# GPS layer: row numbers of every chunk kept, sum buffers given back pair by pair

## The chip, the cores and the metric

The kernel runs on one core of one Trainium2 chip. The metric is the device time of one execution in microseconds (us), as a median over several runs.

## The reference, cut to what matters

A graph of 6250 nodes (256 channels) and 100000 edges, sorted by `dst`. A message network, a linear attention and a slice attention are added to the nodes. The change lies in the message network:

```
xn   = layernorm(x)
row, col = src, dst
filt = silu(edge_attr_20 @ Wf1 + bf1) @ Wf2 + bf2      # 100000 x 256
msg  = xn[col] * filt                                  # 100000 x 256
agg  = segment_sum(msg, row, num_segments=6250)        # a scatter with addition
h    = silu(agg @ Wu1 + bu1) @ Wu2 + bu2
```

## The kernel before, in words

After a first layer norm comes the long stage `messages_and_attention`. It cuts the edges into 98 chunks (`NCH`) of 1024 edges; a chunk is 8 tiles (`ET`) of 128 edges, handled as 4 pairs (`PAIRS`, index `j`). Each engine has its own program, written out by hand, and engines meet only at semaphores. For each pair:

- PE spreads rows of a loaded window of `xn` to the edges (`gather`, L654), makes the filter (`filt`, L664 and L666) and a hidden half of a later pair (`hidden`, L644).
- ACT copies the gathered rows (`copy_rows`, L874), applies silu (L848) and rounds the message to its high half (`high_half`, L867).
- DVE multiplies to the message (`message`, L1018), makes the low half (`low_half`, L981), and compares edge numbers (`indicate` L975, `equal` L993 and L994), which gives a 128x128 mask of edges of the same `src` (`same`) and each edge's rank among its equals (`rank`).
- PE multiplies message halves by the mask (`merge`, L678), so that each edge of a tile has the sum of all edges of that tile with its `src`. ACT copies this to `summed` (`copy_sums`, L855). There are two buffers `summed`, for even and odd chunks, of 8 tiles each.
- POOL adds each tile of 128 rows of 1 KB to a table in HBM with an indirect DMA (`scatter`, L610). Tile `t` goes to table `t % 2` (`TABLES`), and a scatter waits until the one before it on the same table has landed (semaphore `added[k]`, which goes up by 16 for each; `PER` = 4 scatters for each chunk and table). So one scatter per table is under way, two in all.
- The rows that a scatter adds to are in `out_idx`, one column for each tile. DVE makes them once for each chunk, at the end of the chunk before (`out_rows`, L1003 and L1009): the edge's `src`, or a row past the nodes where the edge is not the first of its equals. `src_f` holds `src` as a float, `to_trash` the distance from `src` to that spare row.
- SP loads for later pairs and chunks (`chunk` in the sync program, L503 to L526): `src_row` 512 KB and two `dst_row` of 256 KB for each chunk, a `window` of 128 KB for each pair, `attr` 120 KB for each half chunk. Each load waits until its buffer has been used, mostly by DVE or PE.

Between the pairs stand shares of the linear attention (`work(j)`): scores, gram and output passes of 7 groups. After the stage all engines meet at the block's end, and `update_nodes` begins by loading the tables.

Two places hold the messages' side back when it runs ahead of the scatters. In `out_rows` DVE waits before it writes the row numbers of chunk c until all scatters up to chunk c-2 are down, since `out_idx` has two buffers:

```
dve.wait_ge(added[k], 16 * PER * (c - 1))
```

In `copy_sums` ACT has the same wait, for the same count, before each of the four copies of chunk c, since `summed` has two buffers.

Of the kernel before, what the change touches and what calls it, by code (L numbers as in the profile page):

```python
# [16 lines left out]
I32 = mybir.dt.int32  # L17
ACT = mybir.ActivationFunctionType
X = mybir.AxisListType.X
ds = bass.ds  # L20

P = 128
# [10 lines left out]
ET = 8  # L33
# [8 lines left out]
TABLES = 2  # L42
# [280 lines left out]
def is_first(v):  # L323
    return isinstance(v, int) and v == 0
# [11 lines left out]
def messages_and_attention(nc, sem, sb, g):  # L336
# [16 lines left out]
    PER = ET // TABLES  # L353
# [6 lines left out]
    src_f = sb("src_f", [P, NCH * ET], F32)  # L360
    to_trash = sb("to_trash", [P, NCH * ET], F32)
# [6 lines left out]
    half_f = sb("half_f", [P, 1], F32)  # L368
    base_i = sb("base_i", [1, NW], I32)
    wide_i = sb("wide_i", [1, 1], I32)  # L370
    out_idx = [sb(f"out_idx{p}", [P, ET], I32) for p in range(2)]
    hidT = sb("hidT", [P, 2, CB, HE], F32)
    gathered = sb("gathered", [P, PAIRS, 2, C], F32)
    msg = sb("msg", [P, 2, 2, C], F32)
# [5 lines left out]
    redirect = sb("redirect", [P, ET], F32)  # L380
# [39 lines left out]
    out_ready = sem("e_out_ready")  # L420
    sum_made = sem("e_sum_made")
    sum_ready = sem("e_sum_ready")
    added = [sem(f"e_added{k}") for k in range(TABLES)]
# [57 lines left out]
    with nc.Block() as block:  # L481
# [108 lines left out]
        @block.gpsimd  # L590
        def _(pool):
            def gather(c, j):
                pool.wait_ge(gath_copied, PAIRS * c + j + 1)
                for t in range(2):
                    n = ET * c + 2 * j + t
                    nc.gpsimd.indirect_dma_start(
                        gathered[:, j, t, :], None, g.xn_dram,
                        bass.IndirectOffsetOnAxis(ap=dst_all[:, n:n + 1], axis=0)).then_inc(late_in[j], 16)

            def scatter(c, j):  # L600
                if j == 0:
                    pool.wait_ge(out_ready, c + 1)
                pool.wait_ge(sum_ready, PAIRS * c + j + 1)
                for t in range(2 * j, 2 * j + 2):
                    k = t % TABLES
                    if c == 0 and t < TABLES:
                        pool.wait_ge(g.table_clear[k], 16 * CLEARS)
                    else:
                        pool.wait_ge(added[k], 16 * (PER * c + t // TABLES))
                    nc.gpsimd.indirect_dma_start(  # L610
                        g.sums_dram[k], bass.IndirectOffsetOnAxis(ap=out_idx[c % 2][:, t:t + 1], axis=0),
                        summed[c % 2][:, t, :], None, compute_op=ALU.add).then_inc(added[k], 16)

            nc.gpsimd.memset(attr[:], 0.0).then_inc(cleared, 1)
            pool.wait_ge(win_step, WIN_DONE)
            is_wide = pool.value_load(wide_i[0:1, 0:1], min_val=0, max_val=1)
            with pool.If(is_wide > 0):
                gather(0, 0)
                gather(0, 1)
                for c in range(NCH):  # L620
                    for j in range(PAIRS):
                        n = PAIRS * c + j + 2
                        if n < NW:
                            gather(n // PAIRS, n % PAIRS)
                        scatter(c, j)
            with pool.Else():
                for j in range(PAIRS):
                    pool.sem_inc(late_in[j], 32 * NCH)
                for c in range(NCH):
                    for j in range(PAIRS):  # L630
                        scatter(c, j)
            for k in range(TABLES):
                pool.wait_ge(added[k], 16 * PER * NCH)
# [207 lines left out]
        def _(act):  # L841
# [8 lines left out]
            def copy_sums(c, p, j):  # L850
                act.wait_ge(sum_made, PAIRS * c + j + 1)
                if not (isinstance(c, int) and c < 2):
                    for k in range(TABLES):
                        act.wait_ge(added[k], 16 * PER * (c - 1))
                A.activation(summed[p][:, ds(2 * j, 2), :], sps[:].rearrange("p (t c) -> p t c", c=C),  # L855
                             ACT.Copy).then_inc(sum_ready, 1)

# [19 lines left out]
            def chunk(i, p, last, work):  # L877
                c = 2 * i + p
                for j in range(PAIRS):
                    if j < PAIRS - 1:  # L880
                        copy_rows(c, j + 1)
                    elif not last:
                        copy_rows(c + 1, 0)
                    if j % 2 == 0 and not last:
                        high_attr(c + 1, j // 2)
                    if j == 0:
                        silu(c, 1, 1)
                    elif not last:
                        silu(c + 1, (j - 1) // 2, (j - 1) % 2)
                    high_half(c, j)  # L890
                    if j:
                        copy_sums(c, p, j - 1)
                    elif not is_first(c):
                        copy_sums(c - 1, 1 - p, PAIRS - 1)
                    work(j)
# [59 lines left out]
            copy_rows(0, 0)  # L955
            along(act, chunk, scores, gram, output)
            copy_sums(NCH - 1, 1, PAIRS - 1)

        @block.vector
        def _(dve):  # L960
            V = nc.vector
# [37 lines left out]
            def out_rows(i, p):  # L999

                c = 2 * i + p
                dve.wait_ge(same_ready, PAIRS * c + PAIRS)
                V.scalar_tensor_tensor(out=redirect[:], in0=rank[:], scalar=0.0, in1=to_trash[:, ds(c * ET, ET)],  # L1003
                                       op0=ALU.is_gt, op1=ALU.mult).then_inc(redirected, 1)
                dve.wait_ge(redirected, c + 1)
                if not is_first(i):
                    for k in range(TABLES):
                        dve.wait_ge(added[k], 16 * PER * (c - 1))
                V.tensor_tensor(out_idx[p][:], redirect[:], src_f[:, ds(c * ET, ET)], ALU.add).then_inc(out_ready, 1)  # L1009

            def message(i, p, j):
                c = 2 * i + p
# [8 lines left out]
            def chunk(i, p, last, work):  # L1021
                c = 2 * i + p
                for j in range(PAIRS):
                    message(i, p, j)
                    if j < 2:
                        indicate(c, j + 2)
                    elif not last:
                        indicate(c + 1, j - 2)
                    if not last:
                        equal(i + p, 1 - p, 2 * j)  # L1030
                    low_half(i, p, j)
                    if not last:
                        if j % 2 == 0:
                            low_attr(c + 1, j // 2)
                        equal(i + p, 1 - p, 2 * j + 1)
                    work(j)
                if not last:
                    out_rows(i + p, 1 - p)
# [156 lines left out]
            for t in range(ET):  # L1195
                equal(0, 0, t)
            out_rows(0, 0)
            along(dve, chunk, scores, gram, output)

# [756 lines left out]
def gps_layer(nc, w, x, attr_T, src_rows, src_cols, dst_cols, dst_rows, out):  # L1956
    with ExitStack() as ctx:
# [27 lines left out]
        with ExitStack() as mixing:  # L1985
            sb_mix = lambda *a: mixing.enter_context(nc.sbuf_tensor(*a))
            g.weights = mixing_weights(sb_mix, g)
            g.gate = sb_mix("gate", [P, CB, GC], F32)
            g.zeros = g.gate[:].rearrange("p f n -> p (f n)")[:, 0:ROWS // P * C // CLEARS]
            g.table_clear = [sem(f"table_clear{k}") for k in range(TABLES)]  # L1990
            scoped(first_layernorm, g)
            g.xT = sb_mix("xT", [P, CB, NPAD], F32)
            g.k_max = sb_mix("k_max", [P, CB, 2 * NG], F32)
            g.neg_k_max = sb_mix("neg_k_max", [P, CB], F32)
            g.k_sum = sb_mix("k_sum", [P, CB, 2 * NG], F32)
            g.k_tot = sb_mix("k_tot", [P, CB], F32)
            g.k_inv = sb_mix("k_inv", [P, CB], F32)
            g.bg1f = sb_mix("bg1f", [GH, 1], F32)
            g.wg1f = sb_mix("wg1f", [P, CB, GH], F32)
            g.head_mask = sb_mix("head_mask", [P, P], F32)  # L2000
            g.wqm = sb_mix("wqm", [P, CB, C], F32)
            scoped(messages_and_attention, g)
# [46 lines left out]
```

## Time and profile before

| | us |
|---|---|
| median of 3 runs | 2826.51 |
| lowest, highest | 2817.86, 2831.32 |
| the profiled execution, its own time | 2839.35 |
| its span | 2837.6 |

| engine | busy us | share | instructions |
|---|---|---|---|
| PE | 2088.7 | 74% | 10455 |
| DVE | 1735.1 | 61% | 5026 |
| ACT | 1477.9 | 52% | 2519 |
| POOL | 1423.7 | 50% | 975 |

The shares are averages over the whole span, of which the stage with the messages is about three quarters. A POOL instruction of L610 is the issue of a DMA: its length is the time to issue it, not to land.

### The profile page before, as it was taken

Reading aid. Unit: us, or ns where it says so; the run is one execution under the profiler, and the core shown is the slowest. Engines: PE = TensorE matmul, PEld = TensorE weight load, DVE = VectorE, ACT = ScalarE, POOL = GpSimd, SP = SyncE. Lnnn points to the kernel's source line nnn. Section 1 sums busy time; section 2 is a strip of 40 time slices with the busy share of each in tenths; the row PEclk is TensorE's granted clock in tenths of the full one; section 3 lists DMA queues with packets and bytes.
Section 4 is the critical chain, followed back from the end, with each engine's and each line's share of the span. In section 5 each row is a group of like instructions: output and inputs, shape, how many; then the busy total and the mean of one; then the engine's idle time right before and its main releaser. Section 6 shows DMA issues by size and latency. Waiting matters only on the chain. (4 is left out here: it accounts for less than half of the span.)

```text
span 2837.6 us, 43386 instructions
## 1 busy us (share of the span) xinstructions
PE 2088.7 (74%) x10455; PEld 1704.5 (60%) x10455; DVE 1735.1 (61%) x5026; ACT 1477.9 (52%) x2519; POOL 1423.7 (50%) x975
## 2 busy tenths in 40 slices
PE   0187776677786877787786787878777838789979
PEld 0165665565565755666565666665656537568859
DVE  8266666565565655565665565655656625789945
ACT  1154554454654756566565575746564714346613
POOL 3155665555555565555555555555555543135510
PEclk9998898899898988899998898989898969789979
DMA  8887777777676777777777777777777763300002
GB/s 292 333 178 148 135 154 143 140 147 139 131 155 131 140 135 140 148 149 128 159 143 143 143 159 139 156 133 156 142 150 140 145 116 107 117 1 0 0 16 91
DMA packets 315000, 384.73 MB, mean 136 GB/s; under 512 B 34759, under 2 KB 256135, under 8 KB 314744
## 3 DMA queue, kind: packets, MB, share of 16 engines
q1 hardware_dynamic: 194168, 263.69, 31.8%
q0 software_dynamic: 112896, 102.81, 30.2%
q10 hardware_dynamic: 7744, 16.30, 1.5%
q14 instruction: 149, 1.22, 0.1%
q8 instruction: 43, 0.70, 0.1%
HBM read 234.72 MB, written 147.96 MB: 135 GB/s over the span
## 5 line engine op out<-in xcount | busy, mean ns | idle before, releaser
L610 POOL DMA_INDIRECT sums<-summed,out_idx x784 | 1253.5, 1599 | 972.4 <-DMA sums<-summed,out_idx 737.3
L666 PE MATMUL bank<-wf,hidT 128*128 128x256 f32 x3136 | 878.1, 411 | 0.0
L666 PEld LDWEIGHTS bank<-wf,hidT 128*128 128x128 f32 x3136 | 593.8, 209 | 68.4
L654 PE MATMUL bank<-window,spread 128*128 128x256 f32 x784 | 232.4, 380 | 493.4 <-DVE spread L975 437.6
L1018 DVE TENSOR_TENSOR msg<-bank,gathered 128x512 f32<-128x512 f32 x392 | 270.8, 691 | 372.8 <-PE bank L666 271.9
L848 ACT ACTIVATE hidT<-bank,bf 128x512 f32<-128x512 f32 x392 | 269.2, 687 | 437.6 <-PE bank L644 400.1
L654 PEld LDWEIGHTS bank<-window,spread 128*128 128x128 f32 x784 | 137.1, 204 | 595.2 <-DVE spread L975 426.6
L867 ACT ACTIVATE msg_high<-msg 128x512 fp32r<-128x512 f32 x392 | 246.0, 628 | 400.2 <-DVE msg L1018 392.4
L981 DVE TENSOR_TENSOR msg_low<-msg,msg_high 128x512 fp32r<-128x512 f32 x392 | 271.0, 691 | 113.1 <-ACT msg_high L867 110.4
L664 PE MATMUL bank<-gnn_bf_halves,ones 128*128 128x256 f32 x784 | 318.0, 406 | 0.0
L874 ACT ACTIVATE gathered<-bank 128x512 f32<-128x512 f32 x392 | 232.6, 593 | 75.6 <-issue 43.0
L994 DVE SCALAR_TENSOR_TENSOR rank_scr<-src_row,src_f,earlier 128x128 bf16<-128x128 int32 x784 | 271.3, 346 | 0.0
L644 PE MATMUL bank<-attr_parts,wf_parts 84*128 84x512 f32 x392 | 240.0, 612 | 31.4 <-DVE attr_parts L966 29.5
L993 DVE TENSOR_SCALAR same<-src_row,src_f 128x128 fp32r<-128x128 int32 x784 | 232.4, 296 | 6.7 <-PE bank L678 0.3
L855 ACT ACTIVATE summed<-bank 128x512 f32<-128x512 f32 x392 | 227.8, 581 | 1.1 <-PE bank L678 1.1
L678 PE MATMUL bank<-msg_high,same 128*128 128x256 f32 x784 | 212.9, 293 | 10.4 <-DVE msg_low L981 9.3
L678 PE MATMUL bank<-msg_low,same 128*128 128x256 f32 x784 | 208.0, 287 | 0.0
L1009 DVE TENSOR_TENSOR out_idx<-redirect,src_f 128x8 int32<-128x8 f32 x98 | 16.4, 167 | 307.0 <-DMA sums<-summed,out_idx 301.5
L678 PEld LDWEIGHTS bank<-msg_high,same 128*128 128x128 f32 x784 | 156.4, 199 | 30.5 <-DVE msg_low L981 14.8
L664 PEld LDWEIGHTS bank<-gnn_bf_halves,ones 128*128 128x128 f32 x784 | 163.5, 209 | 13.8
L678 PEld LDWEIGHTS bank<-msg_low,same 128*128 128x128 f32 x784 | 154.3, 197 | 17.9
L975 DVE TENSOR_SCALAR spread<-dst_row,window_row 128x256 fp32r<-128x256 int32 x392 | 150.3, 384 | 0.0
(263 smaller groups left out, 3241.6 us busy)
## 6 DMA issues: line engine op xcount, KB each, us to landing
src_row<-src_rows SPq DMA_DIRECT2D x98, 512.0 KB
dst_row<-dst_rows SPq DMA_DIRECT2D x196, 256.0 KB
window<-xn_halves SPq DMA_DIRECT2D x392, 128.0 KB
attr<-attr_T SPq DMA_DIRECT2D x588, 40.0 KB
xn_stage<-xn_rows SPq DMA_DIRECT2D x21, 896.0 KB
sums<-gate ACTq DMA_DIRECT2D x16, 800.0 KB, 9.3
sums<-summed,out_idx POOLq DMA_INDIRECT x784
part<-sums SPq DMA_DIRECT2D x14, 896.0 KB, 7.2
```

The costliest lines, as they stand in the source:

```text
L610: nc.gpsimd.indirect_dma_start(g.sums_dram[k], bass.IndirectOffsetOnAxis(ap=out_idx[c % 2][:, t:t + 1], axis=0), summed[c % 2][:, t, :], N ...
L644: T.matmul(hps[:], wf1_parts[:, ds(f * P, P)], attr_parts[:, h, :], start=True, stop=True).then_inc(hid_made, 1)
L654: mm = T.matmul(gps[:, ds(t * C, C)], spread[:, j % 2, ds(t * P, P)], window[:, j, :], start=True, stop=True)
L664: T.matmul(out, g.ones2[:], g.bf2[:], start=True, stop=False)
L666: mm = T.matmul(out, hidT[:, j // 2, f, ds((2 * (j % 2) + t) * P, P)], g.wf2[:, f, :], start=False, stop=f == CB - 1)
L678: mm = T.matmul(sps[:, ds(t * C, C)], same[:, p, 2 * j + t, :], half[:, j % 2, t, :], start=k == 0, stop=k == 1)
L848: A.activation(hidT[:, h, f, :], hps[:], ACT.Silu, bias=g.bf1[:, f:f + 1]).then_inc(hid_ready, 1)
L867: A.activation(msg_high[:, j % 2, :, :], msg[:, j % 2, :, :], ACT.Copy).then_inc(high_ready, 1)
L874: A.activation(gathered[:, j, :, :], gps[:].rearrange("p (t c) -> p t c", c=C), ACT.Copy).then_inc(gath_copied, 1)
L981: V.tensor_tensor(msg_low[:, j % 2, :, :], msg[:, j % 2, :, :], msg_high[:, j % 2, :, :].bitcast(F32), ALU.subtract).then_inc(low_ready, 1)
L994: op = V.scalar_tensor_tensor(out=rank_scr[:, t, :], in0=row, scalar=col, in1=g.earlier[:], op0=ALU.is_equal, op1=ALU.mult, accum_out=rank ...
L1018: V.tensor_tensor(msg[:, j % 2, :, :], fps[j % 2][:].rearrange("p (t c) -> p t c", c=C), gathered[:, j, :, :], ALU.mult).then_inc(msg_read ...
```

## The change

The row numbers of all 98 chunks are kept. They are written into `to_trash` itself, whose columns of a chunk are read for the last time by the instruction just ahead (L1003); `out_idx` is now a view of `to_trash` as integers. So DVE's wait on `added` in `out_rows` is gone. ACT's wait in `copy_sums` for pair `j` of chunk c now asks for the scatters of pair `j` of chunk c-2, not for all of chunk c-2. Scatters, tables, loads and all sizes are as before.

```diff
-    out_idx = [sb(f"out_idx{p}", [P, ET], I32) for p in range(2)]
+    out_idx = to_trash[:].bitcast(I32)
...
-                        g.sums_dram[k], bass.IndirectOffsetOnAxis(ap=out_idx[c % 2][:, t:t + 1], axis=0),
+                        g.sums_dram[k], bass.IndirectOffsetOnAxis(ap=out_idx[:, ET * c + t:ET * c + t + 1], axis=0),
...
                 if not (isinstance(c, int) and c < 2):
                     for k in range(TABLES):
-                        act.wait_ge(added[k], 16 * PER * (c - 1))
+                        act.wait_ge(added[k], 16 * (PER * (c - 2) + j + 1))
...
                 dve.wait_ge(redirected, c + 1)
-                if not is_first(i):
-                    for k in range(TABLES):
-                        dve.wait_ge(added[k], 16 * PER * (c - 1))
-                V.tensor_tensor(out_idx[p][:], redirect[:], src_f[:, ds(c * ET, ET)], ALU.add).then_inc(out_ready, 1)
+                V.tensor_tensor(out_idx[:, ds(c * ET, ET)], redirect[:], src_f[:, ds(c * ET, ET)],
+                                ALU.add).then_inc(out_ready, 1)
```

No instruction changes its place. On DVE, at the end of a chunk of the score pass, stands before:

```order
L993 TENSOR_SCALAR same<-src_row,src_f 128x128
L994 SCALAR_TENSOR_TENSOR rank_scr,rank<-src_row,src_f,earlier 128x128
L1051 TENSOR_REDUCE k_max<-bank 128x1 [waits m_k_made]
L1003 SCALAR_TENSOR_TENSOR redirect<-rank,to_trash 128x8 [waits e_same_ready]
L1009 TENSOR_TENSOR out_idx<-redirect,src_f 128x8 [waits e_added1,e_added0,e_redirected]
L1018 TENSOR_TENSOR msg<-bank,gathered 128x512 [waits e_filt_made,e_sum_made,e_late_in0,e_gath_copied]
```

and now, at the same place:

```order
L993 TENSOR_SCALAR same<-src_row,src_f 128x128
L994 SCALAR_TENSOR_TENSOR rank_scr,rank<-src_row,src_f,earlier 128x128
L1049 TENSOR_REDUCE k_max<-bank 128x1 [waits m_k_made]
L1003 SCALAR_TENSOR_TENSOR redirect<-rank,to_trash 128x8 [waits e_same_ready]
L1006 TENSOR_TENSOR to_trash<-redirect,src_f 128x8 [waits e_redirected]
L1016 TENSOR_TENSOR msg<-bank,gathered 128x512 [waits e_filt_made,e_sum_made,e_late_in0,e_gath_copied]
```

The write of the row numbers no longer waits for `e_added0` and `e_added1`; all else is the same, two lines up. On ACT, in the first group of the score pass, the copy of the sums has the same semaphores as before, and a register instruction more ahead of it for each new count:

```order
L867 ACTIVATE msg_high<-msg 128x512 [waits e_msg_ready]
L854 ISA [waits e_sum_made]
L855 ACTIVATE summed<-bank 128x512 [waits e_added1,e_added0]
L874 ACTIVATE gathered<-bank 128x512 [waits e_msg_ready,e_gath_made]
L845 ISA
```

Before, the same place reads:

```order
L867 ACTIVATE msg_high<-msg 128x512 [waits e_msg_ready]
L855 ACTIVATE summed<-bank 128x512 [waits e_added1,e_added0,e_sum_made]
L874 ACTIVATE gathered<-bank 128x512 [waits e_msg_ready,e_gath_made]
```

Behind the copy on ACT stand the next pair's copy of gathered rows, silu and high half.

## Rows read from the trace of the kernel before

**Rows 1.** POOL's scatters: busy us, mean ns | idle; its ACT waits: total, times, longest.

```profile
L610 POOL DMA_INDIRECT sums<-summed,out_idx x784 | 1253.5, 1599 | 972.4 <-DMA sums<-summed,out_idx 737.3 <-ACT summed L855 126.6 <-issue 105.4
...
POOL sums L610 <- ACT summed L855: 126.6, 45, 54.1
```

**Rows 2.** What touches `summed`: duration ns min/median/max, first and last start us.

```profile
L610 POOL DMA_INDIRECT sums<-summed,out_idx x784: 1546/1547/2062, 143.8 to 2313.9; - x196
L855 ACT ACTIVATE summed<-bank x392: 576/579/597, 142.3 to 2294.4; 128x512 f32<-128x512 f32 x196
```

**Rows 3.** That stretch: PE, PEld, DVE, ACT, POOL busy us, clock, DMA, GB/s.

```profile
143.77:2315.46 2171.69, 1640.05 (x7819) 1326.37 (x7817) 1293.13 (x4152) 1236.19 (x2045) 1253.46 (x784) 0.89 0.73 143
```

**Rows 4.** Timeline, end of the stage: start us, us, instruction [idle before <-releaser].

```profile
2294.43 0.60 ACT L855 ACTIVATE summed<-bank 128x512 f32<-128x512 f32 x1 [1.08 <-PE bank L678]
...
2298.42 1.55 POOL L610 DMA_INDIRECT sums<-summed,out_idx  x1 [0.30 <-issue]
...
2302.97 1.55 POOL L610 DMA_INDIRECT sums<-summed,out_idx  x1 [0.80 <-DMA sums<-summed,out_idx]
...
2307.44 1.55 POOL L610 DMA_INDIRECT sums<-summed,out_idx  x1 [1.08 <-DMA sums<-summed,out_idx]
...
2312.05 1.55 POOL L610 DMA_INDIRECT sums<-summed,out_idx  x1 [1.22 <-DMA sums<-summed,out_idx]
...
2323.55 88.69 SPq L1276 DMA_DIRECT2D part<-sums  x14
```

**Rows 5.** Waits of DVE, whole span, at the row numbers.

```profile
DVE out_idx L1009 <- DMA sums<-summed,out_idx: 301.5, 67, 10.9
```

**Rows 6.** Timeline of one such wait.

```profile
1001.27 0.17 DVE L1009 TENSOR_TENSOR out_idx<-redirect,src_f 128x8 int32<-128x8 f32 x1 [10.59 <-DMA sums<-summed,out_idx]
```

**Rows 7.** Timeline behind it: the two scatters nearest to their sums.

```profile
1020.55 0.59 ACT L855 ACTIVATE summed<-bank 128x512 f32<-128x512 f32 x1
1021.42 1.55 POOL L610 DMA_INDIRECT sums<-summed,out_idx  x1 [0.75 <-ACT summed L855]
...
1026.08 0.59 ACT L855 ACTIVATE summed<-bank 128x512 f32<-128x512 f32 x1
1026.94 1.58 POOL L610 DMA_INDIRECT sums<-summed,out_idx  x1 [2.13 <-ACT summed L855]
```

**Rows 8.** Timeline: a long wait put down to ACT, and two copies ahead of it.

```profile
2061.41 0.58 ACT L855 ACTIVATE summed<-bank 128x512 f32<-128x512 f32 x1
...
2081.25 0.59 ACT L855 ACTIVATE summed<-bank 128x512 f32<-128x512 f32 x1
2082.16 2.05 POOL L610 DMA_INDIRECT sums<-summed,out_idx  x1 [3.67 <-ACT summed L855]
```

**Rows 9.** Two stretches, L610 alone: us, POOL busy (x), PE clock, DMA share, GB/s.

```profile
211.00:556.70 345.70, 203.58 (x128) 0.88 0.76 147
930.20:1256.10 325.90, 191.89 (x120) 0.91 0.73 142
```

**Rows 10.** DVE's waits at the row numbers, first stretch, then second.

```profile
DVE out_idx L1009 <- DMA sums<-summed,out_idx: 65.2, 14, 10.6
...
DVE out_idx L1009 <- DMA sums<-summed,out_idx: 28.5, 7, 10.6
```

**Rows 11.** Timeline of PE: first work after the stage, cold and later.

```profile
2335.98 1.97 PE L1288 MATMUL bank<-ident,part 128*128 128x128 f32 x8 [41.59 <-DVE part L1448]
...
2340.88 0.57 PE L1300 MATMUL bank<-agg_low,wu1h 128*128 128x448 f32 x1
...
2360.04 0.36 PE L1300 MATMUL bank<-agg_low,wu1h 128*128 128x448 f32 x1
```

**Rows 12.** Waits of SP's queue for the loads of `attr`.

```profile
SPq L492 <- DVE attr_parts L966: 917.7, 183, 15.8
```

**Rows 13.** Timeline of POOL: the first of 41 rounds in which SP issues no load.

```profile
188.70 1.55 POOL L610 DMA_INDIRECT sums<-summed,out_idx  x1 [1.33 <-DMA sums<-summed,out_idx]
...
196.35 1.55 POOL L610 DMA_INDIRECT sums<-summed,out_idx  x1 [1.34 <-DMA sums<-summed,out_idx]
```

## The prediction

> **What bounds the kernel now.** The page's busy shares point to PE, but they are averages, so I read the waits of the engine at the end of the chain first. The stage with the messages ends when the last scatter has landed: the last sum is copied at 2294.43 us and ends at 2295.03, POOL still has scatters to issue until 2313.9, and only 8 us after that do the loads of the next stage start [rows 2, 4]. While the scatters run, from 143.77 to 2315.46 us, no engine is busy over 76% of the 2171.7 us (PE, 1640) [rows 3].
>
> Is POOL's line of scatters without gaps? It waits 737.3 us for the scatter ahead of it on the same table, 126.6 for ACT's copy of the sums and 105.4 for nothing that is seen [rows 1]; with 1253.5 us of issues that is the whole stretch and the 54.1 us ahead of the first scatter. The reader should doubt the 126.6. Of it 54.1 is that first wait. For the other 44 waits (72.5 us) I counted the copies and the scatters: the scatter at 2082.16 us is the third of its chunk and number 699 of all, so it needs copy number 350, which ended at 2061.99. The view put its 3.67 us down to a copy at 2081.25 that belongs to a later pair and happened to end last [rows 8]. Its real releaser is the landing of a scatter that the view does not show. Of the 392 pairs only two had their sum less than 1 us before the scatter [rows 7]. In the middle case of the 392 (first and last in rows 2) the sum lies ready for 12 us, and the last one for 17.
>
> So the bound is **the chain of scatters, one under way for each table**: 391 steps from pair to pair (I call one a round) in 2312.05 - 143.77 = 2168.3 us [rows 3, 4], 5.55 us each. The messages' side (PE, ACT, DVE) is the faster one and is held back by DVE's wait at the row numbers: 301.5 us in 67 waits [rows 5], each of which ends when a scatter lands and not before [rows 6].
>
> **The change part by part.** The profiled execution took 2839.35 us (span 2837.6 and 1.75 around it); it stands 12.8 us, 0.45%, above the median of 2826.51. The sum is made against 2839.35, and its difference is carried to the median.
>
> 1. DVE's wait is taken away: 301.5 us of idle time on DVE [rows 5]. On the path: 0. What hides it is the stock of sums, four pairs or more at the time of the wait. A message that comes earlier joins a longer line. If that cover were gone (sums just in time), up to the 72.5 us above would be there to gain; that is a rival below.
>
> 2. Sums that came late. The two scatters that were near their sums [rows 7] waited 0.75 and 2.13 us for their copies; with a stock of up to eight pairs in place of about four such a dip is bridged. Bounds: 0 (the scatter ahead may have landed only then) and -2.9 us. I take **-2**, nearer to what is shown as wait.
>
> 3. ACT's wait is finer. For c-2 and pair j it is never later than the old one. It now becomes the place where the messages' side is held back. Behind ACT's copy are queued `copy_rows`, silu and the high half of the next pairs; for these wait DVE's message and PE's filter, and then the next sums. With eight pairs in stock (8 rounds of 5.55 us, 44 us of scatters) a wait of one round reaches POOL never. On the path: 0.
>
> 4. Small things. Two waits less for each chunk on DVE and one register instruction more for some of ACT's copies: both engines stand idle for over 850 us of the stretch [rows 3], so 0. The semaphore counts, scatters and tables are the same: 0. The first scatter waits for the first sum, which no edit touches: 0. At the end the last sums come some 20 us earlier, but the stage ends with the last scatter: 0. PE's pause before the next stage grows from 41.6 us to about 60; its first matmuls there are slow already (0.57 us for a 128x448 one that takes 0.36 later), so a longer pause adds nothing [rows 11].
>
> 5. The loads. Scatters and SP's loads share the DMA engines, which are busy for 0.73 of the stretch [rows 3]. At the very end, with no load left, four rounds start at 2298.42, 2302.97, 2307.44 and 2312.05: 4.54 us each [rows 4], against 5.55 in the mean. So about 1.0 us of each round, 394 us in all, is paid to loads, and their timing is the one thing by which this change can reach the bound. Loads follow DVE (SP waits 917.7 us for DVE's `attr_parts` alone [rows 12]), so they will be spaced differently, a pair at a time. The bytes stay the same. Does the spacing matter? The trace has a test of it: of two stretches [rows 9] the first holds 16 chunks (128 scatters) with 65.2 us of DVE's wait, 4.1 for each chunk; the second holds 15 (120) with 28.5, 1.9 each [rows 10]. The chunks take 345.70/16 = 21.61 and 325.90/15 = 21.73 us. Half the stall, and 0.12 us of 21.7 more. For 98 chunks that is 12 us, and I take it as bound to both sides; my value is **0**, since scatters are under way all the time and a byte that is loaded must be loaded beside one of them.
>
> For the shared access of POOL and DVE: an issue takes 1.547 us in the middle case and at least 1.546, 1.599 in the mean [rows 1, 2]; so all that slows POOL's issues costs 784 x 0.053 = 41.6 us today. DVE's work is the same, so I add 0. The Trainium skill (GPSIMD Engine Reference, 1. Specifications) says that GpSimd shares its SBUF interfaces with VectorE and that instructions of VectorE with two SBUF inputs contend; this speaks against a change that ends DVE's pauses. By that rule, taken at its hardest (the 14% of the stretch in which DVE stood was calm, and is no longer), the sum would be 41.6 x 0.14/0.86 = 7 us longer, 2831.5. The trace bears out only that some issues are longer than others.
>
> Sum: -2 + 0 = -2 us: 2837.4 for an execution like the profiled one, and **2824.5 us** for the median.
>
> **The rivals.**
>
> *A. The sums do come late (faster).* The 44 waits put down to ACT are real, DVE's stall made them, and they go. Price: 126.6 - 54.1 = 72.5 us, so 2754. For it: the view says so, in plain words. Against: the count of copies [rows 8], and a copy that ends 17 us or more ahead in the last rounds [rows 4]. 6%.
>
> *B. The new spacing is kinder (faster).* Held back pair by pair, loads come in smaller groups, just after a round has ended, and more rounds have no load beside them. In 41 rounds SP issues none; the first lasts from 188.70 to 196.35 and the last from 2307.44 to 2312.05 [rows 4, 13], and they take 5.10 us in the mean, since earlier loads still run. If as many became really free at 4.54: 41 x 0.56 = 23 us, so 2803. 12%.
>
> *C. The pauses of the loads go (slower).* While DVE stood, POOL's last round of a chunk had the DMA engines more for itself. With a stall of one pair at a time, some load is queued beside every scatter. It decides if a steady flow costs a scatter more than the same bytes in bursts. Price: the 41 rounds rise from 5.10 to 5.55, 18 us, so 2844.5, 0.6% above the median. For it: the second stretch [rows 9], and that DVE's waits are bunched at the chunk's end. Against: 0.12 us for a chunk is small. The Trainium skill (DMA: Bandwidth & Descriptors, Queues, rings and completion order) says that each DMA engine takes turns between the queue rows that have work, a packet at a time. By that rule a load that waits in a deep queue costs a scatter no more than its turns, while one in every round costs in every round; it would put C's time in place of mine. No row tells turns apart. 20%.
>
> *D. The change does nothing to the pace of the messages either*: ACT's wait holds them back as DVE's did. That is so in the forecast too; the time is the same and it has no chance of its own.
>
> **How the numbers follow.** Within 0.5% of the median, 2812.4 to 2840.6, is about what a measurement of this kernel can tell from no change. The forecast, 2824.5 with its terms' bounds (-2.9 and -12 below, +12 above: 2811.6 to 2838.5), has 62%. B (12%) and A (6%) are faster, 18%; C is slower, 20%. The range reaches from 2798, a little under B, to 2850, a little over C; it leaves out A and the far ends of B and C, with 2 in 10.
>
> **What would show each step.** Right: no wait of DVE on scatters at the row numbers; the idle time appears on ACT at L855, put down to the scatters, with DVE and PE waiting for ACT in turn; the last copy of the sums ends some 35 us or more before the last scatter is issued, not 19; rounds at 5.5 us and the first and last scatter at about 144 and 2314. Wrong: the time between first and last scatter changed by over 14 us. If it fell and POOL's waits for ACT fell by 70, it was A; if rounds became shorter with the same labels, B; if DMA waits of POOL grew, C. A change ahead of the first scatter or after the last would not be explained by anything here.

## The result, and the profile after

The change makes the kernel slower. In the same session the kernel before took 2830.06 us (median of 20 runs), the changed one 2846.99 (20 runs, 2829.37 to 2863.42); the ratio is 1.0063, 95% interval 1.0042 to 1.0083, so about 18 us more. A second measurement (`after_again` below) gives 1.0087, 1.006 to 1.0113. Forecast was 2824.5, no change that can be told, with 20% for slower. A change of 0.6% is small, but both intervals lie above 1.

Single runs of one kernel spread by 30 us and more, so one profile shows where time is spent, but not these 18 us: the profiled execution of the change took 2843.88, 3 under its median, and the one of before 2839.35, 9 over its median of 20.

The first line of the page after and its group of the scatters, and below them the copies of the sums from the view of `summed`:

```profile
span 2842.1 us, 43395 instructions
...
L610 POOL DMA_INDIRECT sums<-summed,to_trash x784 | 1239.4, 1581 | 992.9 <-DMA sums<-summed,to_trash 789.5
...
L855 ACT ACTIVATE summed<-bank x392: 577/597/602, 141.8 to 2286.6; 128x512 f32<-128x512 f32 x196
```

The waits of ACT, then of POOL and DVE, say who is held back now:

```profile
ACT summed L855 <- DMA sums<-summed,to_trash: 707.2, 275, 6.4
...
POOL sums L610 <- DMA sums<-summed,to_trash: 789.5, 445, 5.3
POOL sums L610 <- issue: 124.8, 320, 4.4
...
POOL sums L610 <- ACT summed L855: 61.7, 8, 54.3
...
DVE msg_low L981 <- ACT msg_high L867: 386.8, 237, 6.6
```

The 301.5 us of DVE's wait at the row numbers [rows 5] are gone. ACT waits 707.2 us in 275 waits for scatters in place of DVE's 67 waits, and DVE and PE wait behind it. DVE's wait at `msg_low` for ACT is 386.8 us; before, it was 110.4:

```profile
DVE msg_low L981 <- ACT msg_high L867: 110.4, 72, 3.8
```

POOL waits 789.5 us for its scatters where it was 737.3 [rows 1]. The waits put down to ACT fell from 126.6 us to 61.7, of which 54.3 is the one ahead of the first scatter, and brought nothing.

The end of the stage, by the timeline:

```profile
2317.84 1.55 POOL L610 DMA_INDIRECT sums<-summed,to_trash  x1 [1.10 <-DMA sums<-summed,to_trash]
2319.70 1.56 POOL L610 DMA_INDIRECT sums<-summed,to_trash  x1 [0.30 <-issue]
2329.33 5.95 SPq L1274 DMA_DIRECT2D part<-sums  x4
...
2341.72 1.97 PE L1286 MATMUL bank<-ident,part 128*128 128x128 f32 x8 [58.84 <-DVE part L1446]
```

The last sum is copied 33 us ahead of the last scatter (2286.6 and 2319.7), not 19 [rows 2], and nothing ends sooner for it. PE's pause is 58.8 us where it was 41.6 [rows 11].

In each round POOL issues a scatter for table 0, then one for table 1. From the timeline I counted for 372 rounds how long POOL stood idle ahead of each: before, 1.54 us at table 0 and 0.82 at table 1; after, 1.77 and 0.64. The second scatter now follows more closely behind the first, and the first of the next round comes later. (Over all 391 rounds each of these means, here and in the table below, comes out within 0.04 us of the figure given.) This is the mark by which the experiments below are compared.

### The profile page after: what moved, and what is told of

Same layout as the page of the kernel before. It is cut to its first block and busy times, and to the rows that moved or that the text cites. A ratio compares the mean times of both kernels' runs of the same rounds, so it can differ in the third digit from the quotient of the medians.

```text
span 2842.1 us, 43395 instructions
## 1 busy us (share of the span) xinstructions
PE 2139.0 (75%) x10455; PEld 1696.1 (60%) x10455; DVE 1740.4 (61%) x5026; ACT 1461.9 (51%) x2519; POOL 1409.7 (50%) x975
## 5 line engine op out<-in xcount | busy, mean ns | idle before, releaser
L610 POOL DMA_INDIRECT sums<-summed,to_trash x784 | 1239.4, 1581 | 992.9 <-DMA sums<-summed,to_trash 789.5
L666 PE MATMUL bank<-wf,hidT 128*128 128x256 f32 x3136 | 868.3, 408 | 0.0
L855 ACT ACTIVATE summed<-bank 128x512 f32<-128x512 f32 x392 | 232.6, 593 | 707.7 <-DMA sums<-summed,to_trash 707.2
L981 DVE TENSOR_TENSOR msg_low<-msg,msg_high 128x512 fp32r<-128x512 f32 x392 | 271.6, 693 | 388.0 <-ACT msg_high L867 386.8
L678 PE MATMUL bank<-msg_high,same 128*128 128x256 f32 x784 | 228.8, 312 | 251.3 <-ACT summed L855 242.7
L644 PE MATMUL bank<-attr_parts,wf_parts 84*128 84x512 f32 x392 | 231.7, 591 | 53.6 <-DVE attr_parts L966 51.5
L863 ACT ACTIVATE attr_parts<-attr 84x512 fp32r<-84x512 f32 x196 | 122.4, 625 | 33.0 <-DMA window_ends<-extremes 25.4
```

What stands on the lines that cost most here:

```text
L610: nc.gpsimd.indirect_dma_start(g.sums_dram[k], bass.IndirectOffsetOnAxis(ap=out_idx[:, ET * c + t:ET * c + t + 1], axis=0), summed[c % 2][ ...
L666: mm = T.matmul(out, hidT[:, j // 2, f, ds((2 * (j % 2) + t) * P, P)], g.wf2[:, f, :], start=False, stop=f == CB - 1)
L678: mm = T.matmul(sps[:, ds(t * C, C)], same[:, p, 2 * j + t, :], half[:, j % 2, t, :], start=k == 0, stop=k == 1)
L981: V.tensor_tensor(msg_low[:, j % 2, :, :], msg[:, j % 2, :, :], msg_high[:, j % 2, :, :].bitcast(F32), ALU.subtract).then_inc(low_ready, 1)
```

## Experiments

**Which half of the change costs: `keep_only` and `fine_only`.** In `keep_only` ACT has its old wait:

```diff
-                        act.wait_ge(added[k], 16 * (PER * (c - 2) + j + 1))
+                        act.wait_ge(added[k], 16 * PER * (c - 1))
```

> The change with ACT's old wait: row numbers of all chunks kept, DVE free, but ACT's copies of chunk c wait for all scatters of chunk c-2, so the messages' side is held back once for each chunk and no longer pair by pair. Pacing theory (being held back pair by pair spreads the loads so that one lies beside nearly every scatter): back to the time before, ratio 0.998 to 1.002, rounds at about 5.55 us as before. Depth theory (the cost comes from messages that run eight pairs ahead, however they are held back): stays slower, ratio 1.004 to 1.008. Tile theory (the row numbers read out of a tile of 784 columns, or DVE without its pauses, cost POOL something at each issue): stays slower, ratio 1.005 to 1.008, with longer issues or gaps at the scatters.

`fine_only` is the kernel before with the opposite edit of that line, and DVE's wait kept.

> The kernel before with ACT's finer wait alone; DVE still waits at the row numbers, which comes first. All three theories expect no change: ratio 0.998 to 1.002, no wait of ACT at the copies, DVE's wait at the row numbers near 300 us. Anything else would mean that the finer wait itself costs.

Measured: `keep_only` 0.9984 (0.9966 to 1.0003), `fine_only` 1.0005 (0.9984 to 1.0025). Neither half costs alone. The tile of 784 columns and a DVE without its wait at the row numbers are free, so the tile theory falls. In `fine_only` DVE still waits there (279.8 us) and ACT's copies do not, as expected. The wait view of `keep_only`:

```profile
ACT summed L855 <- DMA sums<-summed,to_trash: 377.4, 77, 9.5
```

77 waits, once for most chunks, against 275 in the change: the messages are held back for as long at a time as before, only by another engine, and the time is that of before. The sums lie ready for 21 us in the middle case, against 12 before, so a deeper stock does no harm of this size.

**How deep: `cap4`, and the change again.** In `cap4` the copy waits for the same pair of the chunk just ahead:

```diff
-                if not (isinstance(c, int) and c < 2):
+                if not is_first(c):
                     for k in range(TABLES):
-                        act.wait_ge(added[k], 16 * (PER * (c - 2) + j + 1))
+                        act.wait_ge(added[k], 16 * (PER * (c - 1) + j + 1))
```

> The change with a stricter wait in ACT: the copy of pair j of chunk c waits for the scatters of pair j of chunk c-1, so the messages are held back pair by pair, but only four pairs ahead in place of eight. Pacing theory: as slow as the change, ratio 1.004 to 1.010, ACT's wait near 700 us or more, sums ready 15 us ahead of their scatters. Depth theory: as before, 0.998 to 1.002. Tile theory: slower, 1.005 to 1.008.

> The change itself once more, beside the others on the same chip, and for a second profile of it: ratio 1.004 to 1.008 by every theory. It shows how far two profiles of one kernel lie apart in their mean round and in the chunks of each pass.

Measured: `cap4` 1.0093 (1.006 to 1.0126), `after_again` 1.0087 (1.006 to 1.0113). With a smaller stock (in the middle case a sum lies ready for 14.5 us in place of 37) the cost is the same, so the depth theory falls too. The waits of `cap4`:

```profile
ACT summed L855 <- DMA sums<-summed,to_trash: 749.0, 283, 6.5
...
POOL sums L610 <- DMA sums<-summed,to_trash: 802.4, 445, 4.9
```

What `cap4` and the change share, and `keep_only` lacks, is that messages are let go pair by pair.

**Pair by pair, or the moment: `phase_early` and `phase_late`.** In the change ACT is let go when the later one of two scatters lands, which is nearly always the one on table 1. `phase_early` adds a wait for the next pair on table 0:

```diff
                     for k in range(TABLES):
                         act.wait_ge(added[k], 16 * (PER * (c - 2) + j + 1))
+                    act.wait_ge(added[0], 16 * (PER * (c - 2) + j + 2))
```

`phase_late` has POOL count its issues, and ACT wait for that count:

```diff
                         summed[c % 2][:, t, :], None, compute_op=ALU.add).then_inc(added[k], 16)
+                pool.sem_inc(issued, 1)
...
+                    act.wait_ge(issued, PAIRS * (c - 2) + j + 2)
```

> The change with ACT's copy waiting besides for the next pair's scatter on table 0, so it is let go when a scatter on table 0 lands and not one on table 1: still pair by pair, at another point of the round, with seven and a half pairs in stock. Spread theory (one pair at a time costs because a load lies beside every scatter, whenever it comes): as slow as the change, ratio 1.006 to 1.010. Phase theory (pair by pair costs because the loads follow the landing on table 1 and always meet the same part of the round): another time than the change by 0.3% or more, either way; the wait at table 0 against that at table 1 (1.75 to 0.65 us in the change, 1.5 to 0.8 before) moves with it.

> The change with ACT's copy waiting besides for a count that POOL raises when it has issued both scatters of the next pair: let go some 3 us later in the round than in the change, behind both issues. Spread theory: 1.006 to 1.010 again. Phase theory: another time than the change by 0.3% or more; if the loads now come when the scatters are half done, nearer to the kernel before, 0.998 to 1.004. POOL raises one count more for each pair, which it can do while it waits.

Measured: `phase_early` 0.9973 (0.9958 to 0.9989), and again 0.9959 (0.9939 to 0.9978): **faster than the kernel before**, and 1.1% (31 us) under the change, by the mean of two measurements of each. It still holds the messages back pair by pair:

```profile
ACT summed L856 <- DMA sums<-summed,to_trash: 691.6, 260, 7.3
...
POOL sums L610 <- ACT summed L856: 461.0, 250, 54.1
POOL sums L610 <- DMA sums<-summed,to_trash: 401.3, 277, 4.3
```

(the waits of `phase_early_again`). ACT's wait is nearly as long as in the change, 691.6 us in 260 waits. So it isn't the spreading, which was rival C's mechanism; it is **the moment in the round at which the messages are let go**. The additional wait also makes the stock a little smaller (32 us of readiness in the middle case for 37), but `cap4` shows that a smaller stock gains nothing. In the first profile of `phase_early` the timeline shows it:

```profile
643.25 0.60 ACT L856 ACTIVATE summed<-bank 128x512 f32<-128x512 f32 x1 [1.33 <-DMA sums<-summed,to_trash]
...
643.88 1.55 POOL L610 DMA_INDIRECT sums<-summed,to_trash  x1 [1.07 <-ACT summed L856]
...
645.73 1.66 POOL L610 DMA_INDIRECT sums<-summed,to_trash  x1 [0.30 <-issue]
...
647.83 0.60 ACT L856 ACTIVATE summed<-bank 128x512 f32<-128x512 f32 x1 [1.91 <-DMA sums<-summed,to_trash]
...
648.48 1.55 POOL L610 DMA_INDIRECT sums<-summed,to_trash  x1 [1.10 <-ACT summed L856]
```

and the same of the change:

```profile
657.33 1.56 POOL L610 DMA_INDIRECT sums<-summed,to_trash  x1 [1.13 <-DMA sums<-summed,to_trash]
...
658.64 0.60 ACT L855 ACTIVATE summed<-bank 128x512 f32<-128x512 f32 x1 [3.04 <-DMA sums<-summed,to_trash]
...
659.20 1.60 POOL L610 DMA_INDIRECT sums<-summed,to_trash  x1 [0.30 <-issue]
...
659.42 0.38 SPq L501 DMA_DIRECT2D window<-xn_halves  x1
```

In the change ACT's copy starts 1.3 us behind POOL's issue for table 0, and here a load is issued 0.8 us later; in `phase_early` the copy starts just ahead of the issue for table 0. The two lines "<-ACT summed" of `phase_early` are false, as in [rows 8]: these scatters need sums that were copied some 30 us before. ACT and POOL are let go by the same landing, ACT's copy ends just ahead of POOL's next start, and the view takes it for the cause: of the 461.0 us only the 54.1 ahead of the first scatter are real, for no other pair had its sum less than 1 us ahead.

`phase_late` came out at 1.008 (1.005 to 1.011). By the expectation on record this is the spread theory's result, and the phase theory's number was missed. The trace shows why it doesn't speak against the moment: the release did not come 3 us later.

```profile
651.12 1.78 POOL L611 DMA_INDIRECT sums<-summed,to_trash  x1 [1.12 <-DMA sums<-summed,to_trash]
...
652.47 0.60 ACT L858 ACTIVATE summed<-bank 128x512 f32<-128x512 f32 x1 [2.44 <-POOLq L614]
...
653.20 1.56 POOL L611 DMA_INDIRECT sums<-summed,to_trash  x1 [0.30 <-issue]
```

ACT is let go by POOL's count (L614) here, 0.73 us before the issue for table 1 shows on POOL, and still during the issue for table 0. Of 372 copies 251 start in the first 2 us of a round, 241 in the change. It is the same moment with one wait more, and the same time. So a second wait by itself is not what helped in `phase_early`. A third moment was not tested.

**Every second pair: `grain2`.**

```diff
-                if not (isinstance(c, int) and c < 2):
+                if not (isinstance(c, int) and c < 2) and j % 2 == 0:
                     for k in range(TABLES):
-                        act.wait_ge(added[k], 16 * (PER * (c - 2) + j + 1))
+                        act.wait_ge(added[k], 16 * (PER * (c - 2) + j + 2))
```

> The change with ACT waiting once for two pairs (at pairs 0 and 2, for the scatters of both pairs of chunk c-2), so it is held back twice a chunk in place of four times. The wait still ends with a landing on table 1, as in the change. Phase theory: some of the loads follow the landing directly and some come a pair later, so the time lies between the kernel before and the change, ratio 1.000 to 1.006, the wait at table 0 between 1.5 and 1.75 us. If it were a matter of spreading alone, also between; a ratio of 1.008 or over speaks against both.

Measured 0.9994 (0.997 to 1.0019). That is just under what was expected: with half the holds the cost is gone, not halved. The mark is more than halfway (1.70 and 0.68 us), so it does not give the time by itself. The repeat of `phase_early` ran beside it.

> The change let go by a landing on table 0, measured once more beside grain2: ratio 0.996 to 0.999, that is 0.9% to 1.1% under the change, with waits of about 1.3 us at table 0 and 1.0 at table 1.

All kernels with two tables and full loads, by the start of the sum copies in the round (372 rounds counted in the timeline of each) and POOL's mean idle time ahead of each issue:

| kernel | copies in the first 2 us | idle at table 0, 1 (us) | ratio |
|---|---|---|---|
| phase_early | 70 | 1.32, 0.99 | 0.9973 |
| phase_early_again | 80 | 1.36, 0.95 | 0.9959 |
| before | 138 | 1.54, 0.82 | 1 |
| fine_only | 148 | 1.50, 0.79 | 1.0005 |
| keep_only | 175 | 1.50, 0.79 | 0.9984 |
| grain2 | 185 | 1.70, 0.68 | 0.9994 |
| after | 241 | 1.77, 0.64 | 1.0063 |
| after_again | 249 | 1.74, 0.65 | 1.0087 |
| phase_late | 251 | 1.81, 0.59 | 1.0080 |
| cap4 | 253 | 1.86, 0.56 | 1.0093 |

The four slow measurements have 241 copies or more in the first 2 us, the two of `phase_early` 80 or fewer. The four in between do not follow the count: `grain2` and `keep_only` have more than the kernel before and are not slower.

The traces also show where the big loads fall. `src_row` (512 KB) is issued 2 to 4 us into a round in 50 of 95 cases before, 20 and 22 in two profiles of the change, 76 and 80 in those of `phase_early`; the `dst_row` loads (256 KB) in 75 of 192, 38 and 39, 90 and 92. The rounds differ with it: before, a round and the next one take together 11.57 us where `src_row` is issued there and 12.18 where it comes in the first 2 us; in the change 11.68 and 12.24. These are counts, not an experiment, and `keep_only` (31 of 95) and `grain2` (25) do not cost what the change does though they lie near it, so they are not the whole of it.

**Through the loads? `light_before`, `light_after`, `light_phase_early`.** After the first chunk only one row each of `dst_row`, `window` and `attr` is loaded, so the messages are made of stale rows; for example:

```diff
-                sp.dma_start(window[:, j, :].bitcast(F32), g.xhl_dram[ds(base, P), :]).then_inc(window_in[j], 16)
+                n = P if is_first(c) else 1
+                sp.dma_start(window[0:n, j, :].bitcast(F32), g.xhl_dram[ds(base, n), :]).then_inc(window_in[j], 16)
```

> The kernel before with almost no loads: of dst_row, window and attr only one row each is loaded after the first chunk, so the messages are computed from stale rows; src_row (512 KB of 1776 KB for each chunk) is loaded whole, and all scatters are made. If loads are what stretches a round from 4.54 to 5.55 us, rounds fall to 4.6 to 4.9 us and the kernel by 250 us or more, ratio 0.87 to 0.93; POOL then waits for sums more often. If the scatters' own latency made the round, it stays near 1.

> The change with the same loads left out (only one row each of dst_row, window and attr after the first chunk). Both loads theories, spread and phase: the gap between the change and the kernel before goes, light_after within 0.3% of light_before or faster than it, since the deeper stock of sums is then worth something. If the gap of 0.6 to 0.9% stays, it was not the loads, but how ACT's wait or the row numbers act on POOL.

> The change with almost no loads once more (only one row each of dst_row, window and attr after the first chunk; src_row whole), as the partner of light_phase_early: ratio 0.926 to 0.931.

> phase_early with the same loads left out (only one row each of dst_row, window and attr after the first chunk; src_row whole). If the phase acts through the loads that follow the release, the gap of 1% between the two phases shrinks with them: within 0.4% of light_after_again. If the phase acts by itself (the copies of the sums, or the messages' engines beside the scatters), the gap stays: 0.8% to 1.2% under light_after_again.

Measured: `light_before` 0.9325 (0.9297 to 0.9352), less of a gain than I had put (0.87 to 0.93); `light_after` 0.9285 (0.9259 to 0.931) and again 0.9275 (0.9251 to 0.9299); `light_phase_early` 0.9229 (0.9204 to 0.9254). What touches `summed` in `light_after`:

```profile
L613 POOL DMA_INDIRECT sums<-summed,to_trash x784: 1546/1547/2067, 141.8 to 2089.1; - x196
```

The mean round falls from 5.56 us in the change to 4.98, 229 us over 391 rounds, for leaving out 1264 of 1776 KB a chunk. The scatters' chain is stretched by loads, as term 5 had it. With these loads gone the change is no longer behind the kernel before but 0.4% ahead. `light_before` is no clean partner for this: with fewer loads its scatters catch up with the sums (15 pairs had theirs less than 1 us before, 3 in the kernel before, the first pair of all among them).

The two moments lie 11 us (0.4%) apart where it was 31, right at the expected bound, and not by noise: the slowest of six runs of `light_phase_early` took 2613.52 us and the fastest of five of `light_after_again` 2615.89. That the gap shrinks fits "through the loads", but does not prove it: ACT is also held less often in the light runs, 157 and 171 times in place of 275 and 260, so part of the shrinking can come from that. What is left may be the 512 KB of `src_row` that is still loaded, or something in the moment itself. So the moment is shown as the cause, and its way through the loads is supported but open in size.

**The bound itself: four tables.** If the landings on two tables are the bound, four should lift it. `tables4` is the change with

```diff
-TABLES = 2
+TABLES = 4
...
-                    for k in range(TABLES):
-                        act.wait_ge(added[k], 16 * (PER * (c - 2) + j + 1))
+                    for t in range(2 * j, 2 * j + 2):
+                        act.wait_ge(added[t % TABLES], 16 * (PER * (c - 2) + t // TABLES + 1))
...
-                a, b = part[s % 2]
-                nc.vector.tensor_tensor(a[:], a[:], b[:], ALU.add).then_inc(agg_ready, 1)
+                a, b = part[s % 2]
+                d, e = extra(s, 0), extra(s, 1)
+                nc.vector.tensor_tensor(a[:], a[:], b[:], ALU.add).then_inc(half_sum, 1)
+                nc.vector.tensor_tensor(d, d, e, ALU.add).then_inc(half_sum, 1)
+                dve.wait_ge(half_sum, 2 * s + 2)
+                nc.vector.tensor_tensor(a[:], a[:], d, ALU.add).then_inc(agg_ready, 1)
```

where `extra` are parts of `res`, which is loaded only after them. `tables4_old` has two small `out_idx` and DVE's wait besides, `tables4_wide_wait` DVE's wait but the wide tile.

> The change with four tables in place of two, so four scatters can be under way: pair 0 and 2 of a chunk use tables 0 and 1, pair 1 and 3 tables 2 and 3; ACT waits pair by pair as in the change; two more tables are cleared at the start (13 MB) and loaded and added in update_nodes. If the chain of landings is the bound, it goes: POOL is then held by its own issues (784 x 1.9 us = 1490 us) or by sums that come late, and the messages' side sets the pace at about 19.5 us a chunk or less: the stage falls by 250 to 350 us, start and update grow by 40 to 80 us together, ratio 0.89 to 0.94. If the DMA engines' load were the bound and not the landings, the ratio stays over 0.97.

> The same four tables with two row-number buffers and DVE's wait for whole chunks, as in the kernel before. With the chain gone DVE's wait should seldom bind: within 0.5% of tables4, either way. If keeping all row numbers is worth something once the scatters are fast, tables4 is ahead by 0.5% or more.

> tables4 with DVE's wait for whole chunks put back, row numbers still in the wide tile. If the wait itself helps (it keeps loads apart, as with two tables), as tables4_old: 0.906 to 0.911. If the wide tile costs, as tables4: 0.913 to 0.918.

> tables4 once more beside it: 0.913 to 0.918 if the gap to tables4_old is a property of the kernel; 0.906 to 0.911 if it was scatter between builds or placements.

Measured: `tables4` 0.9155 (0.9127 to 0.9184), again 0.9149 (0.9124 to 0.9174); `tables4_old` **0.9086 (0.9059 to 0.9113), 2565.34 us**; `tables4_wide_wait` 0.9087 (0.9063 to 0.911). POOL's waits in `tables4_old`:

```profile
POOL sums L610 <- ACT summed L855: 400.7, 162, 82.0
POOL sums L610 <- issue: 203.8, 570, 3.0
POOL sums L610 <- DMA sums<-summed,out_idx: 50.5, 51, 3.5
```

50.5 us of waiting for landings are left of 737.3 [rows 1], and here the 400.7 are true: 307 of 392 sums end less than 1 us before their scatter. Its scatters run from 171.1 to 1993.1 us, 348 us less than in the kernel before, with a start 27 us later for the clearing. The two-table chain was the bound, and all versions with four tables beat both kernels.

The waits for whole chunks are worth 0.7% here, with either tile, so the expectation that `tables4_old` lies within 0.5% of `tables4` was missed. And DVE hardly waits: its largest wait at the row numbers in either is 0.3 us. The gap lies in the gram pass (18.9 us a chunk in `tables4_again`, 18.0 in `tables4_wide_wait`; 16.8 in the score pass of both). From 780 to 1130 us DVE's largest wait for something that the profile does not show is, in `tables4_again`:

```profile
DVE msg L1016 <- issue: 25.5, 13, 5.7
```

and in `tables4_wide_wait`:

```profile
DVE msg L1019 <- issue: 9.8, 18, 0.9
```

The difference, 15.7 us, is of the size of the 19 us between the two kernels. What stops DVE for up to 5.7 us there is open; no run was made for it.

## Why the prediction was wrong, point by point

- *The bound.* Right: the chain of scatters, one for each table. `tables4` took 8.5% off by lifting it, and the unloaded stage in the light runs fell with the loads.
- *Term 1, DVE's wait at no gain.* Right: `keep_only` took it away for 0.9984 (0.9966 to 1.0003).
- *Term 2, late sums, -2 us.* Not to be told at this size; only the first pair is now less than 1 us from its sum. The change did deepen the stock, to 37 us of readiness in the middle case.
- *Term 3, ACT's wait off the path.* Right in what it argued: no wait of ACT reached POOL as a late sum. What it left out is that the wait's end is an event of the scatters' own chain, in most rounds, and that what it sets free comes mostly early in the round (241 of 372 copies in its first 2 us). By term 5 that can reach the path.
- *Term 5, the spacing, taken at 0.* **This is the step that failed.** Moving the hold cost +18 us, or +24 by the second measurement, and the choice of the moment at which it ends, by itself, made 31 us of difference. The price of loads was right in kind (about 1 us a round; leaving out 71% of the bytes of a chunk gave back 0.59). The argument for 0 was that a byte costs the same wherever it falls: the counts of `src_row` above (11.57 against 12.18 us for two rounds) and `phase_early` speak against it, though how much of the 18 us goes through the loads is not settled. The test from two stretches compared two amounts of stall of one kind, let go once for each chunk; it held no case of a hold pair by pair, so it could not bound that. Its bounds of 12 us were no bounds, and the chance that hung on them was too high.
- *Rival C, slower by 18 us.* Sign and size came true, the mechanism did not. Rounds in which SP starts no load did not vanish. By the starts of the issues I count 49 before (5.21 us in the mean; the prediction had 41 at 5.10), and 58 and 47 in the two profiles of the change, with 4.72 and 4.78 us. So these rounds became shorter, and the others longer: 5.71 and 5.64 us where it was 5.59. A pair-by-pair hold at another moment is faster, not slower. The rule on queues that take turns (the Trainium skill, DMA: Bandwidth & Descriptors, Queues, rings and completion order) gives no sign for this: no run here shows the turns, and it does not say when a load hurts.
- *Rival B, kinder spacing, -23 us.* Rounds without a load became shorter, as it said, but the others lost more. A kinder spacing exists: `phase_early` is 0.3% to 0.4% (8 to 12 us) under the kernel before, though not with more such rounds (53 and 46).
- *Rival A, late sums by the wait view.* False, as the count said: 72.5 us of such waits fell to 7.4 and the time rose.
- *Shared access of POOL and DVE, +7 us by the rule* (the Trainium skill, GPSIMD Engine Reference, 1. Specifications). Not seen, but not tested either: issues take 1.581 us in the mean, where it was 1.599. The premise that DVE's pauses end was wrong. They moved from the row numbers to `msg_low`; DVE is busy 1293.1 us of the stretch before and 1298.5 after, so its idle time is the same.
- *The signs named beforehand.* Those for "right" came (DVE's wait gone, ACT's there, the last copy 33 us ahead), and the time was slower all the same: they showed where the hold is, not what it costs. The sign for C came too, POOL's DMA waits grew by 52 us, but those put down to ACT fell by 65. The first-to-last distance grew by 6 us only, from 2170.1 to 2176.5, under the 14 named as sign of being wrong: one execution of each does not show a shift of half a per cent.

The 62% for "no change" were too high. A term set to 0 by argument, and one mechanism of unknown sign, should have given more to both sides. That C's price of 18 us is what was measured is luck.

## What to carry to other kernels

When a chain of transfers is the bound, moving the back-pressure from one engine to another is not free, even if no work comes late: ask which event ends the wait, and what it sets off at which point of the chain's own round. Here a hold pair by pair that ended on the landing on table 1 cost 0.6% to 0.9%, and one that ended on table 0 gained 0.3% to 0.4%. Before tuning such a hold, lift the bound: two more tables took off 9.1%, more than twenty times as much.

## What the runs showed of the hardware that was not expected

- One wait more on ACT, which changes the moment (and the stock a little, which `cap4` shows to gain nothing), moved the whole kernel by 1.1% (1.0063 and 1.0087 against 0.9973 and 0.9959).
- In the wait view of a kernel whose engines are let go by the same landing, 407 us of POOL's 952 us of idle time (461.0 less the 54.1 ahead of the first scatter) are put down to an instruction that had no part in it. A count of producers and consumers in the timeline settles such a line.
- With four tables a wait that hardly ever holds (0.3 us at most) still made the kernel 0.7% faster. Most of the difference shows as stops of DVE in the gram pass whose cause is open.
